# Sixteen steps as the body of the local layers' loop, and a prefetch hint for the jump back on each engine

## What is computed

```python
x = L0_attn_x
x = _layernorm(x + _L0_attn_ref(x, ...))
for i in range(DEPTH):                                   # DEPTH = 6, inside _L0_ffn_ref
    x = attn_layer(shift_tokens(x), Wqkv[i], q_scale[i], k_scale[i], Wo[i]) + x
    x = ffn_layer(shift_tokens(x), ln_g[i], ln_b[i], W1[i], b1[i], W2[i], b2[i]) + x
```

## Time and profile before

| | before |
|---|---|
| median of 3 runs | 4710.56 us (4701.91 to 4711.07) |
| the profiled execution | 4716.59 us |
| its span in the profile | 4714.8 us |
| PE busy in the span | 4147.4 us, 88% |
| DVE, ACT, POOL busy | 62%, 56%, 59% |
| mean granted clock of TensorE | 0.957 of full speed |
| attention stage | to about 919 us |
| local layers | about 919 to 4672 us |

### The profile page before, as it was taken

One profiled execution on the slowest core, in us unless ns is written; L12 is line 12 of the kernel. 1 busy time (PEld: TensorE's weight loads), 2 busy tenths in 40 slices (PEclk: granted clock), 3 DMA queues, 4 the chain that ended last, 5 costly groups with the idle time before them and its releaser, 6 DMA issues. The chain is left out here.

```text
span 4714.8 us, 163642 instructions
## 1 busy us (share of the span) xinstructions
PE 4147.4 (88%) x67078; PEld 2777.6 (59%) x67078; DVE 2916.1 (62%) x4217; ACT 2622.4 (56%) x4417; POOL 2799.6 (59%) x3584
## 2 busy tenths in 40 slices
PE   5878788689999999999999999999999999999994
PEld 2434344356666666666666666666666666666663
DVE  5565656566666666666666666666666666666664
ACT  2535354446556565665656655656566555665662
POOL 0000000177777777777777777777777777777771
PEclk9979788899999999999999999999999999999997
DMA  0000000112222122222222222222222222222223
GB/s 27 3 15 2 16 16 3 42 45 58 69 71 72 51 69 65 72 57 64 65 69 64 56 66 69 77 53 69 65 72 56 65 65 69 64 56 65 69 66 79
DMA packets 284548, 258.85 MB, mean 55 GB/s; under 512 B 122872, under 2 KB 258509, under 8 KB 271149
## 3 DMA queue, kind: packets, MB, share of 16 engines
q1 hardware_dynamic: 283820, 248.14, 19.7%
HBM read 117.63 MB, written 29.77 MB: 31 GB/s over the span
## 5 line engine op out<-in xcount | busy, mean ns | idle before, releaser
L785 DVE TENSOR_TENSOR products<-bank_d,table 128x1024 f32<-128x1024 f32 x772 | 938.1, 1216 | 716.5 <-ACT sq L612 711.8
L908 POOL TENSOR_TENSOR products<-products 128x2048 f32<-128x2048 f32 x192 | 870.4, 4533 | 263.1 <-DVE products L785 263.1
L411 PE MATMUL bank_d<-w_qkv,xT 128*128 128x512 f32 x1544 | 805.6, 625 | 25.2 <-DVE products L785 14.2
L612 ACT ACTIVATE sq<-bank_d 128x512 f32<-128x512 f32 x772 | 467.8, 606 | 484.8 <-PE bank_d L411 474.6
L945 POOL TENSOR_TENSOR qk_rot<-products,rnorm 128x2048 f32<-128x2048 f32 x192 | 695.4, 3622 | 15.0 <-POOL rnorm L927 14.6
L783 DVE TENSOR_REDUCE ss<-sq 128x16 f32<-128x1024 f32 x386 | 468.7, 1214 | 240.3 <-ACT sq L612 240.3
L952 POOL TENSOR_TENSOR prob<-prob,inv_sum 128x1024 f32<-128x1024 f32 x192 | 365.1, 1902 | 407.3 <-DVE inv_sum L765 407.3
L872 POOL MEMSET ident<- 128x128 f32 x1 | 0.2, 204 | 914.6 <-POOLq L1062 914.6
L1489 DVE TENSOR_REDUCE part_max<-s_max 128x1 f32<-128x512 f32 (+3 forms) x768 | 398.3, 554 | 150.7 <-PE s_max L1238 101.2
L457 PE MATMUL bank_a<-ident,qk_rot 128*128 128x128 f32 x3072 | 412.6, 290 | 69.6 <-issue 64.0
L457 PEld LDWEIGHTS bank_a<-ident,qk_rot 128*128 128x128 f32 x3072 | 366.9, 149 | 150.4 <-issue 103.0
(11 more groups left out here) (168 smaller groups left out, 7551.9 us busy)
## 6 DMA issues: line engine op xcount, KB each, us to landing
v_back<-v SPq DMA_DIRECT2D x96, 768.0 KB, 5.5
w_qkv<-in_Wqkv_dram SPq DMA_DIRECT2D x25, 1024.0 KB, 5.0
v_back<-v SPq DMA_DIRECT2D x192, 128.0 KB, 5.5
w_qkv<-in_Wqkv_dram SPq DMA_DIRECT2D x25, 512.0 KB, 5.5
xs<-x_layers SPq DMA_DIRECT2D x194, 64.0 KB, 2.1
w_o<-in_Wo_dram SPq DMA_DIRECT2D x24, 512.0 KB, 6.0
xr<-x_layers SPq DMA_DIRECT2D x96, 128.0 KB, 2.2
x<-x SPq DMA_DIRECT2D x96, 128.0 KB, 1.8
```

The source lines that it names most:

```text
L411: nc.tensor.matmul(bank[:, :], xT[:, P * a:P * (a + 1)], w_qkv[:, col:col + 512], start=True, stop=True).then_inc(d_filled if i < 8 else a ...
L612: nc.scalar.activation(sq[j % 2][:, 8 * c:8 * c + 8, :], bank_d[slot][:, :].rearrange("p (h d) -> p h d", d=DH), ACT.Square).then_inc(squa ...
L785: nc.vector.tensor_tensor(products[:, a, head:head + 8, :, :].rearrange("p h r (o d) -> p h r o d", o=2), bank[:, :].rearrange("p (h r d) ...
L908: link(nc.gpsimd.tensor_tensor(products[:, a, :, 0, :], products[:, a, :, 0, :], products[:, a, :, 1, :], ALU.add))
```

## The change

The written-out part of the local layers becomes one whole layer (four batches, 16 steps) and the loop runs over layers 1 to 5 with 16 steps as its body. Both loops, this one and the one over batches in the attention stage, are made with `hint_back_edge=True`, which puts one instruction (BRANCH_PREFETCH_HINT) at the head of the body of each engine that names the jump at its end. Nothing inside a step is changed.

```diff
         def rounds(eng, step_fn, last_fn=None):
-            for p in range(POS):
-                step_fn(Step(0, p))
-            with eng.Fori(1, ROUNDS) as f:
+            for b in range(BATCH):
                 for p in range(POS):
-                    step_fn(Step(f, p))
+                    step_fn(Step(b, p))
+            with nc.Fori(1, DEPTH, engines=[eng.engine], hint_back_edge=True) as layer:
+                for b in range(BATCH):
+                    for p in range(POS):
+                        step_fn(Step(BATCH * layer + b, p))
             for t in range(PAIRS, PAIRS + MAX_LAG):
                 step_fn(Step(ROUNDS, t - PAIRS))
...
         def batches(eng, body):
             body(0)
-            with eng.Fori(1, BATCH) as b:
+            with nc.Fori(1, BATCH, engines=[eng.engine], hint_back_edge=True) as b:
                 body(b)
```

## The result

The changed kernel takes 4665.86 us (median of 5 runs, 4657.07 to 4683.02) against 4708.40 (4701.91 to 4711.07): ratio 0.9915, interval 0.9893 to 0.9936. It gained 43 us where 100.2 were forecast, and lies outside the range given. The profiled execution took 4670.98 us, with a span of 4669.2.

What follows compares the result with a forecast made beforehand. TensorE, busy 88% of the span, was taken as the bound, standing idle at each loop jump. 81.0 + 17.2 + 2.0 = 100.2 us off the 4710.6 us median gave 4610 us, range 4594 to 4637.

Steps and rivals of the forecast that it cites:

- The step that failed: Code to be fetched in the layers' loop: TensorE's stream stalls only at the jump, so added fetching costs 0.
- the present stream runs without a gap: Argument against the starved-fetch rival: TensorE's code now streams at 34 instructions a us without a gap.
- the prediction's price of a jump: Layers' loop: each jump back costs a round 4.5 us, from round lengths, with ends 3.3 and 5.2.
- Jumps that go: Layers' loop closed 4 times instead of 22: 18 jumps at 4.5 us go, 81.0 us gained.
- Rounds should take 149.2 us throughout: Sign to look for in the layers: rounds without a jump take 149.2 us; otherwise the prediction is wrong.
- Jumps that stay: The layers' four remaining jumps, hinted, cost 0.2 us each in place of 4.5: 17.2 us gained.
- The attention stage: Its loop's two jumps back, with a working hint, give 1.2 + 0.8 = 2.0 us; nothing without.
- Packets of code: Sign to look for: the queue of instructions carries 610 to 670 packets, against 581 before.
- The hint does nothing: Rival, chance 0.16: 18 jumps go, the four that stay remain at 4.5 us or slightly more; 4632 us.
- Streaming with an armed hint starves the fetch: slower: Rival, chance 0.04: the hinted target crowds out TensorE's next code blocks in the loop; about 4920 us.

Runs made afterwards that it cites:

- the small copies: The changed kernel with the three v to v_back copies of a step cut to the first 64 of 1024 columns: 4592.05 us, ratio 0.9761.
- the four-step loop: The kernel before, its body of four steps and 22 jumps kept, with the hint alone added to both loops: 4731.22 us, ratio 1.0062.
- section 1: The changed kernel, sixteen steps in the loop's body, without the hints on both loops: 4742.72 us, ratio 1.0091 against the kernel before.
- section 6: The kernel before with TensorE's loop head at place 199 of its 256-instruction block in place of 135: 4972.26 us, ratio 1.0555.

## Why the prediction was wrong

**The step that failed** is "TensorE's stream of some 20 packets a round shows no stall but the jump: its 22 long idle times at 'issue' are all at the seam ... I take 0." It fails twice. First, is one line's row. The same view of the kernel before, from 1070 to 4550 us, goes on:

```profile
PE bank_a L498 <- issue: 23.9, 23, 1.2
PE bank_d L411 <- issue: 9.4, 7, 2.5
PE scores L476 <- issue: 8.9, 10, 1.5
```

These 42.2 us fall at one place modulo 256 as well (117 to 121 behind the loop's head); I read the row that I was looking for. The same reading stands in the rival's "the present stream runs without a gap", which is wrong too. Second, a stream that runs well at four fixed places says nothing of sixteen steps at all places. The sum had no term for where the code lies.

**The accounts.** In the kernel before, the 22 jumps are 22 x 4.5 = 99 us of the 149.7 us of excess; about 50 us was other waiting. In the changed kernel the jumps are 4 x 1.3 = 5 us of 103.7, which leaves about 98. So some 94 us of jumps went and about 48 us of late code came: 46 less in the steps, and 43 in the time. The split is an estimate: the 4.5 us are the prediction's price of a jump with what follows it, the 1.3 us are the bare jump.

**Jumps that go, 81.0 us:** about right. With the steps back at their old places and four unhinted or unhelped jumps of 3.5 us left, the kernel gains 89 us (73 where the hint of the attention stage is missing too, whose batches are then 7 us longer). A round without a jump in it takes 147.9 us there, the mean of 19 by the stores; 149.2 was forecast. "Rounds should take 149.2 us throughout" is wrong for the changed kernel: its layers take 604.8 to 611.5 us, 151.2 to 152.9 a round.

**Jumps that stay, 17.2 us:** mis-sized. I took 0.2 us, they are 1.3 us, so 4 x (4.5 - 1.3) = 12.8 us by this sum. A hinted jump is not always as quick as one whose target is at hand; where it stands in its block decides, and the data in the way (0.5 us at the same place with the small copies).

**The attention stage, 2.0 us:** about right. The jumps fell from 3.7 and 3.3 to 0.4 and 0.3 us, and the two batches that follow them are 3.1 us shorter together, but the first began later in this execution: the first store comes at 1079.3 us, against 1077.3.

**Packets of code:** I wrote 610 to 670 for a queue that carries TensorE's code alone. It fell to 550, as 18 jumps no longer fetch a head of a body; the others' code is on q14 (147, then 198).

**The rivals.** "The hint does nothing": wrong, though it is so in the four-step loop. "Streaming with an armed hint starves the fetch: slower": the late blocks came, "in mid-step" as the text says, but not by the hint: without it they are longer, up to 5.5 us, and with neither hint nor loop the excess is 166.4 us. The rival had the right place and the wrong mechanism, and with 0.04 it was priced as if only the hint could bring it. The place of code in its block deserved a rival of its own, since the change shifts all of TensorE's instructions.

**The borders of blocks.** The pauses at one place modulo 256 and the packets of 16 KB show blocks of 256 instructions, each fetched while the one before it runs. The Trainium skill says the same, in "Runtime: NRT & Kernel Launch", section "Instruction fetch mechanics". The same section of the Trainium skill calls the cost of crossing such a border "mostly hidden". Here a border costs up to 3.7 us of idle time in the changed kernel and up to 5.5 us in that of section 1, and section 6's kernel, in a bad place, takes 265 us more; the measurement decides.

**What stays open:** by what means TensorE's armed hint lets a block in the middle of the body be fetched about 2 us sooner. The traces show that it does and at which places, not how. And the largest remaining cost, the copies of `v_back`, was only cut by leaving values out; another way to build them was not tried.

## What to carry to other kernels

Look at a busy engine's idle times at "issue" on all lines, and count its instructions modulo 256 at each: where they agree, the time hangs on where the code lies, and any edit that shifts it, an added loop or a removed jump, is worth what its places are worth before it is worth anything else. So compare variants only with the hot code held at one place, and choose the place by measuring steps at several: the same instructions took from 4596 to 4727 us written out, and 4706 to 4972 in a loop. An idea that no run here tested: put large copies where the engine is in long instructions, not just ahead of a stretch of short ones.

## What the runs showed of the hardware

- A fetch of TensorE's next block waits behind data: 3.8 us from entering the block until the packet moved, while data held 94.5% of the DMA engines. TensorE went through those 256 instructions in 3.1 us (3518.72 to 3521.8). With the copies cut to a sixteenth the waits at late blocks were 1.3 us at most.
- After a packet had landed, TensorE took another 1.2 to 1.8 us to go on, in the 18 pauses of the changed kernel.
- A pause of 3.1 us was followed by 6 us at a granted clock of 0.51 (1.2 GHz), with 1.00 (2.4 GHz) before it: the step lost 6.2 us, twice the pause.
- What the prefetch hint did for TensorE's jump went by where the jump stood: 3.5 us at 8 instructions behind a border, 1.3 at about 120 (0.5 with the small copies), 0.4 at about 190. Beside its jump it moved the fetch of ordinary blocks forward at some places (25.3 against 27.4 us into a step, medians of 10), worth 77 us in one kernel and at most 0.3% in another.
- On the other four engines the hint brought the head of a sixteen-step body 0.4 to 0.5 us after the jump in place of 2.4 to 5.2, and the kernel's time did not change by it.
- A forward jump that only aligns code costs little: TensorE's at line 247 took 0.3 us in the median, 20 times.
